# Order of work in the routed experts' turns: VectorE, ScalarE, GpSimd and the load queue

## The reference

```
x = layernorm(x)                       # 800 tokens, 256 wide
coef[t, e] = weight of expert e for token t (8 of 64 experts for each token, 0 elsewhere)
g = x @ Wg[e];  u = x @ Wu[e]          # 256 -> 128
h = silu(g) * u * coef[:, e]
moe_out += h @ Wd[e]                   # 128 -> 256
shared = silu(x @ SWg) * (x @ SWu) @ SWd
out = x_before + moe_out + shared
```

## Time and profile before

| | us |
|---|---|
| median of 3 runs | 726.96 |
| profiled execution | 726.52 |
| its span, first to last instruction | 724.7 |
| PE busy | 618.8 |
| ACT busy | 398.6 |
| DVE busy | 388.7 |
| POOL busy | 249.0 |
| first gate product of the routed experts | 556.98 |
| last down product ends | 712.9 |

### The profile page before, as it was taken

How to read it: one execution, slowest core, us unless ns; L and a number is a source line. 1 busy time by engine, 2 the same in 40 slices (tenths; PEclk the granted TensorE clock), 3 DMA queues, 4 the chain that set the end, 5 groups by cost and what they waited for, 6 DMA issues and landing times.

```text
span 724.7 us, 14858 instructions
## 1 busy us (share of the span) xinstructions
PE 618.8 (85%) x4634; PEld 488.5 (67%) x4635; DVE 388.7 (54%) x1148; ACT 398.6 (55%) x952; POOL 249.0 (34%) x326
## 2 busy tenths in 40 slices
PE   3999799999750999989999999999498599999994
PEld 1877466666450888986788756666366588888884
DVE  5222567777643111117988745454864566666662
ACT  1444699989741333335576696876251355555552
POOL 5011455555308000002100000000044588888883
PEclk9999699999955899999999999999679799999999
DMA  6118100000076288403110010000024666666665
GB/s 148 46 31 259 37 2 2 2 2 2 1 241 240 91 290 287 152 30 93 33 47 6 1 50 1 1 1 2 0 91 107 178 172 171 178 170 180 174 172 132
DMA packets 71339, 69.28 MB, mean 96 GB/s; under 512 B 10892, under 2 KB 64873, under 8 KB 71162
## 3 DMA queue, kind: packets, MB, share of 16 engines
q1 hardware_dynamic: 64256, 59.99, 27.2%
q0 software_dynamic: 4272, 6.55, 4.5%
q10 hardware_dynamic: 2762, 2.11, 1.0%
HBM read 56.99 MB, written 11.64 MB: 95 GB/s over the span
## 4 chain that ended last, share of the span: by engine, by line
PE 52%; ACT 11%; POOL 10%; issue 10%; DVE 10%; DMA 3%; SPq 1%; DVEq 1%; POOLq 0%; ACTq 0%
ACT probs L769 4%; PE psum L1112 4%; PE psum L1125 4%; PE psum L617 3%; PE psum L631 3%; PE psum L1599 3%; PE psum L1621 3%; PE psum L1608 3%; PE psum L708 3%; DMA v_all<-in_L_ffn_W_dram 3%; PE psum L1647 2%; PE psum L698 2%; POOL sum_dram L2370 2%; POOL we_low L2355 2%; POOL h_low L2363 2%
## 5 line engine op out<-in xcount | busy, mean ns | idle before, releaser
L769 ACT ACTIVATE probs<-probs,negmax 100x361 f32<-100x361 f32 x128 | 68.9, 587 | 10.8 <-POOL probs L814 10.7
L822 DVE TENSOR_SCALAR_CACHE_REDUCE probs<-psum 100x361 f32<-100x361 f32 x128 | 60.7, 531 | 19.1 <-PE psum L698 19.1
L708 PEld LDWEIGHTS psum<-ident,probs 100*128 100x128 f32 (+1 forms) x384 | 39.7, 157 | 27.6 <-issue 19.8
L708 PE MATMUL psum<-ident,probs 100*128 100x100 f32 (+1 forms) x384 | 48.1, 264 | 11.4 <-ACT probsT L777 4.8
L1153 ACT ACTIVATE kT_all<-psum,kT_all 128x128 f32<-128x128 f32 x88 | 25.1, 368 | 52.0 <-PE psum L1112 52.0
L2185 PE MATMUL psum<-xT_high,we_high 128*128 128x400 f32 x128 | 45.4, 355 | 9.0 <-DVE v_all L2437 8.2
L814 POOL TENSOR_SCALAR probs<-probs 100x722 f32<-100x722 f32 x64 | 50.6, 790 | 5.1
L1112 PE MATMUL psum<-kT_all,v_all 128*128 128x128 f32 x352 | 44.0, 286 | 7.5 <-DMA v_all<-in_L_ffn_W_dram 2.9
L1112 PEld LDWEIGHTS psum<-kT_all,v_all 128*128 128x128 f32 x352 | 42.6, 201 | 10.4 <-issue 6.6
L2070 POOL TENSOR_TENSOR xT_low<-kT_all,xT_high 128x1600 fp32r<-128x1600 f32 x1 | 3.6, 3571 | 130.9 <-ACT xT_high L2047 130.9
L2186 PE MATMUL psum<-xT_low,we_high 128*128 128x400 f32 x128 | 45.0, 351 | 0.0
(11 more groups left out here) (419 smaller groups left out, 1630.5 us busy)
## 6 DMA issues: line engine op xcount, KB each, us to landing
v_all<-in_L_ffn_W_dram SPq DMA_DIRECT2D x16, 1024.0 KB, 7.9
kT_all<-coefT_dram SPq DMA_DIRECT2D x18, 400.0 KB, 4.5
v_all<-in_L_ffn_Wg_dram SPq DMA_DIRECT2D x34, 128.0 KB
v_all<-in_L_ffn_Wu_dram SPq DMA_DIRECT2D x34, 128.0 KB
v_all<-in_L_ffn_Wd_dram SPq DMA_DIRECT2D x34, 128.0 KB
ctx_nat<-in_ctx_dram SPq DMA_DIRECT2D x16, 192.0 KB
xs_dram<-zeros SPq DMA_DIRECT2D x1, 2048.0 KB, 7.7
rank_rows<-rank_dram SPq DMA_DIRECT2D x18, 100.0 KB
```

Source lines behind the costliest of these rows:

```text
L708: last = nc.tensor.transpose(pT_ps[0:rows[t], t, hh * NQ:(hh + 1) * NQ], probs[:, n % NPB, hh, t * P:t * P + rows[t]], ident[0:NQ, 0:NQ])
L769: last = nc.scalar.activation(row, row, ACT.Exp, bias=negmax[:, n % NPB, hh:hh + 1])
L822: last = nc.vector.tensor_scalar(probs[:, n % NPB, hh, 0:NKV], psum[0:NQ, n % 2 * 2 + hh, 0:NKV], -CLAMP, None, ALU.max, ALU.max, accum_ou ...
```

## The change

On VectorE one `split_small` moves ahead of `hidden(i, 0)` and the other stands alone between `hidden(i, 0)` and `hidden(i, 1)`, small expert 0 first; the low part of the last half of h (`hidden(i, 1, 1)` on GpSimd before) becomes `last_low` on VectorE. ScalarE splits small expert 0 first. GpSimd does both halves of `hidden(i, 0, ...)` before `add_second`, and waits in the first for the `h1_ready` count of the turn before. SyncE loads the small experts' weights for turn i + 1 in turn i, behind the dense ones, and those of turn 0 ahead of the loop; the rank rows' wait on `row_of_ready` goes. ScalarE waits once after the loop for the small weights that were loaded beyond the last turn.

```diff
@@ sp_experts1
-        def load_rank(i, k, n, first=False):
-            if not first:
-                sp.wait_ge(row_of_ready, 3 * i + k - 2)
+        def load_rank(k, n):
...
         total = sp.value_load(n_used[0:1, 0:1], min_val=0, max_val=E1)
+        load_small(0, 0, small_at(sp, total, 0, 0))
         sp.wait_ge(ranks_stored, 16)
         for k in range(2):
-            load_rank(0, k, small_at(sp, total, 0, k), True)
+            load_rank(k, small_at(sp, total, 0, k))
         sp.wait_ge(coefT_stored, 16)
         for p in range(2):
             load_coef(0, p, dense[p])
+        load_small(0, 1, small_at(sp, total, 0, 1))
...
-                        for k in range(2):
-                            load_small(i, k, small_at(sp, total, i, k))
                         dense = [load(i + 1, p) for p in range(2)]
                         load_coef(i + 1, 0, dense[0])
+                        load_small(i + 1, 0, small_at(sp, total, i + 1, 0))
                         for k in range(2):
-                            load_rank(i + 1, k, small_at(sp, total, i + 1, k))
+                            load_rank(k, small_at(sp, total, i + 1, k))
+                        load_small(i + 1, 1, small_at(sp, total, i + 1, 1))
                         load_coef(i + 1, 1, dense[1])
@@ act_experts1
-                        split_small(i, 1)
+                        split_small(i, 0)
                         silu(i, 0, 0)
                         high(i, 0, 0)
                         silu(i, 0, 1)
-                        split_small(i, 0)
+                        split_small(i, 1)
...
+        for k in range(2):
+            act.wait_ge(ws_loaded[k], 24 * total + 48)
@@ pool_experts1, hidden
             pool.wait_ge(y1_in_psum, 4 * n + 4)
+            if p == 0 and half == 0:
+                pool.wait_ge(h1_ready, 4 * i + 2)
@@ pool_experts1, the loop
                         gather(i)
-                        hidden(i, 0, 0)
+                        for half in range(2):
+                            hidden(i, 0, half)
                         add_second(i)
-                        hidden(i, 0, 1)
-                        for half in range(2):
-                            hidden(i, 1, half)
+                        hidden(i, 1, 0)
@@ dve_experts1
         def split_small(i, k):
-            dve.wait_ge(ws_high_ready, 2 * i + 2 - k)
+            dve.wait_ge(ws_high_ready, 2 * i + k + 1)
...
+        def last_low(i):
+            n = 2 * i + 1
+            dve.wait_ge(h1_high_ready, 2 * n + 2)
+            dve.wait_ge(y1_in_psum, 4 * n + 4)
+            dve.wait_ge(h1_ready, 2 * n + 3)
+            nc.vector.tensor_tensor(h1_low[1][:, HT:2 * HT], h1T[:, HT:2 * HT], h1_high[1][:, HT:2 * HT].bitcast(F32),
+                                    ALU.subtract).then_inc(h1_ready, 1)
...
+                        split_small(i, 0)
                         hidden(i, 0)
-                        for k in (1, 0):
-                            split_small(i, k)
+                        split_small(i, 1)
                         hidden(i, 1)
                         for k in range(2):
                             rows_low(i, k)
+                        last_low(i)
```

## The result

| | before | after |
|---|---|---|
| median, us | 726.09 | 729.24 |
| profiled execution, us | 726.52 | 730.36 |
| its span, us | 724.7 | 728.6 |

The medians are of one comparison on one chip (8 runs each). The ratio is 1.0041, with an interval from 1.0025 to 1.0058: 2 to 4 us more. That is clear of no change, though the middle of the interval lies under the half per cent that the prediction set as its bound. The forecast was 727.9. It came close with one term of its sum badly wrong and with two errors in another that cancelled, and the profile shows which.

What follows compares the result with a forecast made beforehand. The prediction took one VectorE and ScalarE chain of 18.32 us a turn as the bound: -1.8 (first turn) + 7 x 0.15 + 1.7 (end) = +0.95 on 726.52, plus 0.44: 727.9 us, own range 725.5 to 730.5, whole range 718.5 to 732.5.

Steps and rivals of the forecast that it cites:

- The turn: VectorE/ScalarE chain of a steady turn: 1.2 us won undisturbed, waits for GpSimd added back, net +0.15 a turn.
- The second case: ws_low(0) waits 1.31 us until both GpSimd down splits are over; ws_low(1) then meets no h_low: +0.1 a turn.
- the first: ws_low(0) gets in between GpSimd's two down splits, waiting 0.56 us; ws_low(1) waits 0.8 for h_low(0,0): +0.16 a turn.
- what wins once wins always: VectorE against GpSimd: since turns repeat closely, whichever goes first does so every turn; argued against rival 1, no size.
- ws_low(1) alone between H01 and H10: VectorE, from second to third h product's end: 2.12 us instead of 4.02 with one split there, a gain of 1.90.
- rivals 1 and 2: Steady turns: one wait missed, -0.64 a turn, 722.2 us (chance 0.24); no waits, full 1.2 a turn, 718.1 (0.14).
- First turn: Loop start: small weights no longer awaited, but row search and number loads decide; -1.8 us, bounds -0.5 and -3.
- add_second: GpSimd, issued at t = 10.7 instead of 8.41, landing 5.2 to 6.1 later; usually in time by 0.3 to 0.5 us.
- rival 3: add_second lands too late for VectorE's keep_rows and ScalarE's os_rows(1): 0.7 us a turn more, 732.8 us (chance 0.14).
- GpSimd's scatter issue: add_second's issue on GpSimd, 2.15 us beside ws_low: new place wins nothing by the page, about 0.5 by the rows.
- SyncE's queue. Nothing: SyncE's reordered loads: rank rows about 2 us later but needed at about 17, dense loads no earlier; no cost.
- the last term of the sum: Loop's end: SyncE's x load waits for the last add_second's landing, 2.15 us later minus 0.4 slack: +1.7 us.

Runs made afterwards that it cites:

- e2: Changed kernel with GpSimd's gather moved ahead of its two down splits: 736.62 us, ratio 1.0141 to the kernel before.
- e3: Changed kernel with VectorE's ws_low(0) put back behind hidden(0), so both splits stand together: 733.47 us, ratio 1.0105 to the kernel before.
- e7: Kernel before with the small experts' weights loaded a turn ahead, small expert 1 first: 726.31 us, ratio 1.0002 to the kernel before.
- e6: Changed kernel with the small experts' weights loaded at the head of their own turn, as before: 726.53 us, ratio 0.9997 to the kernel before.
- e4: Kernel before with the final x load issued by ScalarE instead of SyncE: 731.24 us, ratio 1.0073 to the kernel before.
- e5: Changed kernel with gather ahead of down splits, GpSimd's first h_low waiting for ws_low(1), rank rows ahead of small loads: 727.71 us, ratio 1.0025 to before.
- e9: Gather first, first h_low behind ws_low(1), rank rows early, plus small expert 0's loads ahead of the dense ones, on changed kernel: 726.31 us, 1.0004 to before.
- e1: Changed kernel with the final x load issued by ScalarE instead of SyncE: 729.75 us, ratio 1.0052 to the kernel before.
- e8: Changed kernel with both ws_low behind hidden(0) and add_second back between the two h_low(0,*): 727.47 us, ratio 1.0014 to the kernel before.

## Why the prediction was right and wrong

The number was right: 729.24 lies within the forecast's own range (725.5 to 730.5). The sum was not: +0.95 was forecast for the profiled execution, +3.84 came. That the median fell in the range is in part luck.

- *The turn* (7 x 0.15 forecast, 7 x 0.16 measured): the mechanism was right, the size came out by two errors that cancelled. The second case came in six turns (H00 5.82 against 5.96), the first in one, so "what wins once wins always" didn't hold. In those six the wait was 1.19, forecast 1.31. But the gain of ws_low(1) alone between H01 and H10 was 1.67, not 1.90: 2.12 was forecast for that stretch, though the prediction itself gives 2.33 to 2.34 from one half to the next, and no half in these traces follows in less. Undisturbed, the change wins 1.0 a turn and not 1.2, and with a wait of 1.19 a turn gets 0.20 longer (forecast +0.1); the odd turn is 0.05 shorter. Turns of 17.1, and the prices of rivals 1 and 2 that rest on 1.2, were out of reach.
- *The price of a wait* was taken too low: the outer bounds let a split stand behind one operation (1.31 and 0.8), and e2 and e3 show 2.1 behind two. It did no harm only because, in the six turns, at ws_low(1)'s ask the second h_low wasn't ready, as the working of the second case had it.
- *TensorE*: it stops 1.33 before gate_up(1) and no longer at the second down product, as forecast; the end of that wait bought nothing.
- *First turn*: -1.5, forecast -1.8; the search at 561.57, the split at 565.84 and H00 at 568.06 are each inside their stretch.
- *last_low*: 0.57 in VectorE's idle time (633.71), and no one waits for it. *add_second*: it lands 4.8 to 5.1 after its issue at t = 10.24, and keep_rows doesn't wait for it; rival 3 had no case.
- *GpSimd's scatter issue*: 1.61 in its new place instead of 2.15. The Trainium skill infers ("SBUF — State Buffer", Who interferes with whom) that such a VectorE operation doesn't hold descriptor making, so that the new place would win nothing. The trace disagrees: an issue that starts while a two-input VectorE operation runs is longer by about what is left of it (a gather at 624.04 takes 1.51 beside the ws_low that ends at 624.65, else 1.02). In the first turn of before the scatter's issue starts 0.16 ahead of one (571.84, the ws_low at 572.00) and takes 1.60.
- **The step that failed is "SyncE's queue. Nothing", and with it the last term of the sum** ("SyncE loads x once the last add_second has landed", +1.7). The term measured +4.2, and its cause was another. The landing (708.4 by the forecast, 708.65 in the trace of before) and SyncE's free moment (708.9, where its wait instruction took 17 ns) lay together in that trace, and I took the one for the other; the changed kernel's trace (708.9 and 712.0) and e7 part them, and e6 shows that it was the loads. The queue was looked at only for what *uses* its loads late, not for what stands behind them. In the last turn they serve no turn at all, but the final load waits for them. Before, small loads stood at the turn's head, beside SyncE's wait for GpSimd's splits.

The other 0.7 of the 4.2 is in the load itself: from issue to the final sum 8.40, against 7.70 where it still had 0.4 of slack. Over all runs with one load this stretch was 6.6 to 8.4 (e7 6.59, e4 6.81, e5 7.05, e9 7.81), and in e3 9.0. What sets it stays open, and with e1's end, unmoved by a later issue, it leaves open how much of the 3.5 a shorter queue alone would win back. A version that skips the small loads of the last turn wasn't tried.

What another order on GpSimd is worth is shown by e5 and e9: 0.6 us a turn against before. The change reached none of it, since it won 1.0 on the chain, 0.98 of it the old wait behind one h_low, and lost 1.19 in the down splits.

## What to carry to other kernels

A load moved a turn ahead in a loop also stands in the last turn, in front of whatever its queue issues after the loop: read the queue's last issue beside the landing before you name one as the cause, for two ends within 0.3 us can hide each other. Before you price the gain of a shorter stretch, look for the next chain under it: here ScalarE's, 0.2 us away. When an operation on VectorE with two SBUF inputs asks beside GpSimd, price it by the row of GpSimd operations that are ready, and keep that short: GpSimd waits for it (e5), or its big operations don't stand back to back (e8). Where a last sum waited for one large load, halves with a semaphore each won about 2 us here.

## What the runs showed of the hardware

- *A wait through a whole row.* A two-input VectorE operation of 0.95 us took 1.9 with one ready GpSimd operation in its way, 2.13 through the rest of two splits, 2.98 through two h_low. The Trainium skill ("SBUF — State Buffer", Who interferes with whom) says that the order of issue decides who blocks. By that rule e2's split, which asks just before the down splits end, would have gone next, at 1.1 in all. The trace has 2.98: the two h_low that were ready went first. But in one turn in seven of the changed kernel VectorE did get in between two splits (641.04), and it got in ahead of the one-element product each time. What lets it in is open.
- *Leaving a loop.* From SyncE's last issue in the loop to the first behind it 2.4 to 3.2 us passed (2.41 in e6, 2.44 before, 2.93 after, 3.17 in e7); on ScalarE 1.8 from its last copy's end. The loop is two nested ones, and the outer one is written for four passes of which only the first has work here. SyncE's branches of the outer loop's line behind its last issue, in the changed kernel:

```profile
L1934 SPq COMPARE_BRANCH  x4: 40/45/58, 709.7 to 711.8; - x4
```

So most of it is three empty passes at 0.7 us each (0.5 in the kernel before). What a kernel without them would win wasn't tried.
